# A row of constants per expert, loaded to each expert tile and added by VectorE, and made in the first layer's scan

## What is computed

```
def _L3_ffn_ref(x, W1, b1, W2, b2, Wr, br):
    E, D, H = (8, 128, 512)
    B, S = (4, 512)
    indices = jnp.argmax(softmax(x @ Wr + br), axis=-1)
    out = jnp.zeros_like(x)
    for i in range(E):
        mask = (indices == i)[..., None]
        xi = x * mask
        h = jax.nn.relu(xi @ W1[i] + b1[i])
        out = out + (h @ W2[i] + b2[i])
    return out
```

## Time and profile before

| | before |
|---|---|
| median of 3 runs | 2878.7 us |
| lowest, highest | 2875.16, 2884.09 us |
| the profiled execution, time | 2880.42 us |
| the profiled execution, span | 2878.8 us |
| granted TensorE clock, mean | 0.869 |
| PE busy, whole span | 2282.3 us (79%) |
| DVE, ACT, POOL busy | 1646.9, 1246.8, 728.6 us |

### The profile page before, as it was taken

The page is one execution under the profiler, slowest core; times in us unless marked ns, Lnnn a source line. Parts: engine busy times, 40 slices in busy tenths (PEclk is TensorE's granted clock), DMA queues, the critical chain, the costliest instruction groups (busy, mean ns, idle before and its releaser), DMA issues. The chain is left out here.

```text
span 2878.8 us, 44649 instructions
## 1 busy us (share of the span) xinstructions
PE 2282.3 (79%) x15600; PEld 1322.9 (46%) x15600; DVE 1646.9 (57%) x3299; ACT 1246.8 (43%) x1904; POOL 728.6 (25%) x872
## 2 busy tenths in 40 slices
PE   3888888852899989999755389999999788786485
PEld 2555555541344444444342134444443676454375
DVE  6676767630577747657039277777776243554202
ACT  2343434320366656665620036565656443232143
POOL 1435343441010101000000223232322112664422
PEclk8898888875799999999855589999999999996688
DMA  2111100012011101110010302121211696111075
GB/s 61 38 53 53 46 2 2 2 26 73 2 50 42 53 27 28 50 36 20 1 31 0 101 19 74 49 74 48 74 50 38 221 315 218 42 41 27 30 253 172
DMA packets 138636, 183.14 MB, mean 64 GB/s; under 512 B 26378, under 2 KB 112603, under 8 KB 133311
## 3 DMA queue, kind: packets, MB, share of 16 engines
q1 hardware_dynamic: 97629, 134.91, 15.9%
q0 software_dynamic: 13696, 32.02, 3.5%
q10 hardware_dynamic: 27126, 13.75, 1.7%
HBM read 127.86 MB, written 52.21 MB: 63 GB/s over the span
## 5 line engine op out<-in xcount | busy, mean ns | idle before, releaser
L1711 DVE TENSOR_REDUCE a_mpart<-a_mx 128x1 f32<-128x512 f32 (+3 forms) x1216 | 741.8, 656 | 293.2 <-PE a_mx L1482 156.7
L1625 ACT ACTIVATE a_prob<-a_st 128x1024 f32<-128x1024 f32 (+3 forms) x768 | 607.2, 812 | 493.1 <-PE a_st L1508 372.2
L1482 PE MATMUL a_mx<-a_ka,a_qa 96*128 96x512 bf16 (+3 forms) x1536 | 432.4, 342 | 30.7 <-DVE a_mpart L1711 14.1
L1505 PE MATMUL a_st<-a_qa,a_ka 96*128 96x512 bf16 (+3 forms) x1536 | 417.5, 334 | 30.6 <-ACT a_prob L1625 22.0
L1523 PE MATMUL a_acc<-a_prob,a_v_aug 128*9 128x512 f32 (+3 forms) x3072 | 322.0, 495 | 0.0
L1482 PEld LDWEIGHTS a_mx<-a_ka,a_qa 96*128 96x128 bf16 x1536 | 141.7, 100 | 317.7 <-DVE a_mpart L1711 172.0
L1409 POOL DMA_INDIRECT x_rows<-l_xn,l_slots x128 | 125.4, 980 | 404.9 <-ACT a_prob L1625 395.0
L1505 PEld LDWEIGHTS a_st<-a_qa,a_ka 96*128 96x128 bf16 x1536 | 146.3, 100 | 137.1 <-ACT a_prob L1625 38.2
L1508 PE MATMUL a_st<-w_mask_t,identb 128*128 128x128 bf16 x1024 | 208.8, 223 | 0.0
L2076 PE MATMUL t_psu<-t_xsT,t_w 128*128 128x128 f32 x960 | 149.2, 289 | 25.4 <-DMA t_w<-in_l_experts 17.4
L1485 PE MATMUL a_mx<-w_mask_q,identb 128*128 128x128 bf16 x768 | 165.8, 225 | 0.0
(11 more groups left out here) (444 smaller groups left out, 4129.8 us busy)
## 6 DMA issues: line engine op xcount, KB each, us to landing
t_w<-in_l_experts SPq DMA_DIRECT2D x160, 192.0 KB, 4.2
t_w<-in_l_experts SPq DMA_DIRECT2D x40, 514.0 KB
a_qa<-q_parts_dram SPq DMA_DIRECT2D x96, 192.0 KB
a_ka<-k_parts_dram SPq DMA_DIRECT2D x96, 192.0 KB
x_rows<-zeros SPq DMA_DIRECT2D x25, 512.0 KB, 3.6
t_xs<-x_rows ACTq DMA_DIRECT2D x40, 256.0 KB, 4.6
y_rows<-t_y POOLq DMA_DIRECT2D x40, 256.0 KB
q_parts_dram<-a_parts SPq DMA_DIRECT2D x24, 256.0 KB, 3.0
```

What stands on the lines that cost most here:

```text
L1482: ins = pe.matmul(to, qa[G % NQ][:, h0 + k, qi * P:(qi + 1) * P], ka[G % NQ][:, h0 + k, lo:hi], start=not masked_first, stop=k == per - 1 ...
L1505: ins = pe.matmul(to[:, lo:HALF], ka[G % NQ][:, h, j * P:(j + 1) * P], qa[G % NQ][:, h, ch * HALF + lo:(ch + 1) * HALF], start=True, stop= ...
L1625: act.activation(prob[:, v % NP_, 2 * pair:2 * pair + 2, lo:HALF], sring[s % 2][:, :, lo:HALF], ACT.Exp, scale=1.0 if alibi else scale).th ...
L1711: dve.tensor_reduce(mpart[:, G % 2, h0:h0 + per, qi, piece], slot[:, 0:per * width].rearrange("p (k w) -> p k w", k=per), X, ALU.max).then ...
```

## The change

The constants are made at the end of the first layer's scan, and handed to the experts in another way.

- In the scan, SP loads the W2 of experts 0 to 3 (1024 KB) into a third of `lmat` that the scan no longer needs, b1 and b2 beside it; after job `("base", 0)` has read it, the W2 of experts 4 to 7. ACT takes the relu of b1 (event `above`, position 57.4). PE makes the eight own rows in two jobs of 16 calls, `("base", 0)` at position 58.0 and `("base", 1)` at 60.1, and DVE copies each job's 512 numbers out of its PSUM slot. At 60.8 DVE adds b2, sums over the experts and subtracts, which gives for each expert `base - own_e` (three instructions on one partition). SP stores the 8 rows to `base_dram`. The store of the row numbers into `x3_rows` moves to here as well, and stands before the end of the scan's block.
- `route` of layer 2 loses all its work on constants, and `layer_norm` the three loads. The `ones_row` and `l3_base` tiles are gone.
- In the experts of layer 3 the call L2089 and the load of the negated row are gone. Instead SP loads for each tile the 512 bytes of its expert's row to all 128 partitions (`to_broadcast([P, D])`, 64 KB written per tile), two such loads behind the weights of tiles 3, 5 and 7 and two more at the end. Before the two, SP waits until the pair's addition in the iteration before is done. DVE adds these rows in place of `l3_base`, after a wait for their loads.

```diff
+        put(NTILES - 6.6, ("above",))
+        put(NTILES - 6.0, ("base", 0))
+        put(NTILES - 3.9, ("base", 1))
+        put(NTILES - 3.2, ("base_sum",))
...
+                    sp.wait_ge(wlast_s, NTILES // HT - 2)
+                    for done in (mm_s, gs, cd_s, st_s):
+                        sp.wait_ge(done, NTILES - NT)
+                    sp.dma_start(l3_w2, a["l3_w2"][:, 0:E3 // 2]).then_inc(w2_in[0], 16)
+                    sp.dma_start(above[:], a["l3_b1"]).then_inc(base_in, 16)
+                    sp.dma_start(l3_b2, a["l3_b2"].rearrange("(o e) d -> o e d", o=1)).then_inc(base_in, 16)
+                    sp.wait_ge(*made("base", 0))
+                    sp.dma_start(l3_w2, a["l3_w2"][:, E3 // 2:]).then_inc(w2_in[1], 16)
+                    sp.wait_ge(base_s, 1)
+                    sp.dma_start(base_dram.rearrange("(o e) d -> o e d", o=1), base_rows).then_inc(base_stored, 16)
...
+                        elif kind == "base":
+                            pe.wait_ge(above_s, 1)
+                            pe.wait_ge(w2_in[e[1]], 16)
+                            for k in range(E3 // 2):
+                                for m in range(CH):
+                                    ins = pe.matmul(slot[0:1, 0, k * D:(k + 1) * D], above[:, e[1] * E3 // 2 + k, m:m + 1], l3_w2[:, k, m],
+                                                    start=m == 0, stop=m == CH - 1)
+                            ins.then_inc(ring_made, 1)
...
+                        elif kind == "base_sum":
+                            dve.wait_ge(*freed_of("base", 1))
+                            dve.wait_ge(base_in, 32)
+                            link(dve.tensor_tensor(l3_b2, l3_b2, own, ALU.add))
+                            link(dve.tensor_reduce(own_sum[:], l3_b2.rearrange("p e d -> p d e"), X, ALU.add))
+                            dve.tensor_tensor(base_rows, own_sum[:].unsqueeze(1).to_broadcast([1, E3, D]), own, ALU.subtract).then_inc(base_s, 1)
...
-                        pe.matmul(psb, ones8[:], b2[:], start=True, stop=False)
-                        for e in range(E3):
-                            for m in range(CH):
-                                pe.matmul(pso[e // 4][:, e % 4 * D:(e % 4 + 1) * D], b1[:, e, m:m + 1], w2[:, e, m],
-                                          start=m == 0, stop=m == CH - 1)
-                                ins = pe.matmul(psb, b1[:, e, m:m + 1].to_broadcast([P, P]), w2[:, e, m],
-                                                start=False, stop=e == E3 - 1 and m == CH - 1)
...
                             e = bass.ds(chosen[k], 1)
                             sp.dma_start(w[:, k], weights[e].rearrange("e p k -> p (e k)")).then_inc(w_loaded[k], 16)
-                            if not gated:
-                                sp.dma_start(negc[:, k], negc_dram[e]).then_inc(w_loaded[k], 16)
+                            if bases is not None and k >= 3 and k % 2:
+                                base_pair(it, k // 2 - 1, chosen)
+                        if bases is not None:
+                            base_pair(it, pairs - 1, chosen)
...
-                        pe.wait_ge(w_loaded[k], (16 if gated else 32) * (it + 1))
+                        pe.wait_ge(w_loaded[k], 16 * (it + 1))
...
-                            pe.matmul(to, ones_row[:], negc[:, k], start=True, stop=False)
...
-                            dve.tensor_tensor(y[:, half, at:at + 2], made_y, base[:].unsqueeze(1).to_broadcast([P, 2, D]), ALU.add
-                                              ).then_inc(y_out, 1)
+                            dve.wait_ge(base_loaded[q], 32 * (it + 1))
+                            dve.tensor_tensor(y[:, half, at:at + 2], made_y, base[:, 2 * q:2 * q + 2], ALU.add).then_inc(y_out, 1)
```

98 lines of the change are left out of this document (43 added, 55 removed).

## The result

| | before | after |
|---|---|---|
| median (20 runs each) | 2873.93 us | 2884.32 us |
| lowest, highest | 2867.80, 2884.09 us | 2870.34, 2891.82 us |
| ratio after / before, 95% interval | | 1.003 (1.0016 to 1.0043) |
| the profiled execution: time, span | 2880.42, 2878.8 us | 2888.05, 2886.4 us |
| granted TensorE clock, mean | 0.869 | 0.865 |

The change makes the kernel slower by 0.3%, some 9 us: between 4.6 and 12.4 us by the interval. The forecast was 4.7 us faster, with no measurable change as the likeliest class. The 2884.3 us lie inside the stated range of 2865 to 2886, but by luck: the range was set from a kernel before of 2878.7 us, and over more runs this takes 2873.9. As a change, the range was -13.7 to +7.3 us, and +8.6 lies outside it.

The account below looks back on a forecast made before the run. TensorE was taken to bound the experts and the scan's end, with DMA 19% behind in the experts. Experts -12.0, scan +8.1, normalization -0.8 and routing 0 gave -4.7 us: 2874.0 us against a median of 2878.7, range 2865 to 2886.

Parts of the forecast that it names:

- What bounds the kernel: Layer 3's experts and the first scan's end: TensorE bounds, 20.00 of 20.00 us in an expert iteration, DMA share 0.81.
- By TensorE alone the stage gains 14.8 us.: Layer 3's experts: removing the 0.42 us call from 40 tiles gives 16.8 us, less 2.0 at the loop's turns.
- I take 0.26, between the two queues' prices, since they are counted in packets of this very size.: Layer 3's experts: each 64 KB row load costs 0.26 us of all DMA engines, with ends of 0.2 and 0.6.
- The second rival: Layer 3's experts: dear rows make them DMA-bound and the kernel slower, 2893 us at 0.8 us per row; chance 0.09.
- The halfway case: Rows at 0.36 to 0.6 us, or a scan costing 10 us or more: 0 to +8 us, about 2882; chance 0.15.
- 32p - 11.4: Whole kernel: change in us if a row costs p us of all DMA engines; the sign turns at p = 0.36.
- But the slots let SP run up to 8 tiles ahead, and some 1.1 us per iteration is partly taken from that lead.: Layer 3's experts: SP's lead partly covers the DMA excess, so the gain is 12 us, between 10.4 and 14.8.
- VectorE's and SP's new waits, "nothing": Layer 3's experts: VectorE's wait for the rows and SP's wait for the earlier addition of the pair cost nothing.
- signs of being wrong: Iterations at or above 20 us, `l_hmax` less than 4 or more than 10 us late, or VectorE waiting for `t_base`.
- The scan, 8.1 us: First scan's end: two jobs add 3.7 and 3.9 us and a copy 0.5, making `l_hmax` and the end 8.1 us later.
- "Nothing" for `base_sum`: First scan's end: its three one-partition instructions, 3.7 us in all, lie behind `l_hmax` beside POOL's work and cost nothing.
- Normalization -0.8, routing 0: Layer 2: three loads less in the normalization give -0.8 us (0 to -0.8); removing the routing's 65 constant calls gives 0.

Follow-up runs that it names:

- both together: Rows read from 128 places, constants made in layer 2's routing, input loads issued two tiles earlier, against the kernel before: ratio 0.993, median 2852.08 us, stage 88.52 us.

## Why the prediction was wrong, point by point

- **What bounds the kernel.** Right: TensorE in the experts and at the scan's end. What it left out was how near the third party was. The inputs' load landed after 4.4 us and had 6.3 us until TensorE wanted it (issued at 2784.46, transposed at 2790.72 in the trace of before), and the text never priced it.
- **"By TensorE alone the stage gains 14.8 us."** Too low. The call's 0.42 us was right, but a tile without it is 0.6 us shorter, so 40 tiles give some 24 us, and an iteration needs some 15.2 us of TensorE (20.03 less 8 x 0.60), not 17.2. The kernel "both together" has iterations of 16.4 us. The 15.2 are below the text's own 16.2 us of the DMA engines per iteration, so by its sum these would bound the stage even with rows that cost nothing.
- **"I take 0.26, between the two queues' prices, since they are counted in packets of this very size."** The failed step. A row costs 0.53 us by its packets, since all are read from one DRAM row; from 128 places it costs 0.22, near the 0.23 that the text read from the input loads. So the likeness of size holds for pieces from different places, and not for these. The second rival named the reason ("all 128 pieces are read from the same 512 bytes in DRAM"). The halfway case, with rows at 0.36 to 0.6 and 0 to +8 us, came nearest to what happened, and had a chance of 0.15. By the text's formula, 32p - 11.4, the price of 0.53 gives +5.6 us where 0.26 gives -3.1, so engine time alone explains some 9 of the 16 us by which the forecast missed. In the runs the dear rows cost more, 18.7 us of the stage (118.0 against 99.2 with the rows from 128 places). With rows from 128 places the stage is 11 us shorter than before, close to the forecast's 12, but by luck: TensorE's saving is larger and the late inputs take a part of it back.
- **"But the slots let SP run up to 8 tiles ahead, and some 1.1 us per iteration is partly taken from that lead."** The second failed step, to which the rest belongs. The lead belongs to the weights. The inputs have no such lead, and what fills the DMA engines by bursts delays them: they land 10.0 us after issue. The runs with rows in one iteration and with none show it: 110.5 and 99.5 us, against some 86 (110.2 - 24) by TensorE's saving alone. The first iteration, which was to gain 3.4 us, lost 0.8.
- **VectorE's and SP's new waits, "nothing".** VectorE waited once for rows, for 2.8 us, one of the text's own signs of being wrong; so was an iteration above 20 us. A wait for `t_w` in each iteration, which it expected of a stage bound by the DMA engines, didn't come.
- **What a stall costs** was not in the sum at all: in the stall shown above, the clock at 0.50 behind it doubled it.
- **The scan, 8.1 us.** The term was near, 6.98 at the end of the stage, and `l_hmax` 6.8 late. Jobs 3.65 instead of 3.9 us, the copy 0.68 instead of 0.5. "Nothing" for `base_sum` was wrong in kind: it doesn't queue, it slows POOL, by 1.7 us in two pairs.
- **Normalization -0.8, routing 0**: the first as forecast, the second within 0.4 us.
- **The sum.** 5.4 + 7.0 - 0.8 = +11.6 us by the stages of the profiled executions, against +8.6 (4.6 to 12.4) by the runs. The miss of 16.3 us between -4.7 and +11.6 is 17.4 in the experts' term, -12 against +5.4, less 1.1 in the scan's.

## What to carry to other kernels

A transfer that spreads one row over the partitions is not priced by its bytes or pieces: where it is repeated in a loop that uses the DMA engines at 80%, as here, try writing the row out once to 128 places and reading these. What the removal of a call saves is read from the start of the group before it to the start of the group behind it, in a kernel with and one without it, and not from its own time alone. Before a step of the bounding engine is shortened, list every load that must land within the loop with its time from issue to use; the one with the least slack can become the bound, as the inputs did here, and a stall can cost TensorE its clock too. Work placed on a full engine's path (the scan) cost nearly its full length, 7.0 us for two jobs of 3.65 and a copy of 0.68; where it was hidden before, its removal gave nothing.

## What the runs showed of the hardware that was not expected

- One load of 64 KB in 128 pieces of 512 bytes takes 0.34 to 0.57 us of all 16 DMA engines (means over the 40 rows of a stage) when all are read from one 512-byte row, and 0.22 when they are read from 128. Most packets take 27 ns either way; of those from one row 8 to 22% take over 200 ns on the mean. The input loads' pieces of 516 bytes take 0.24 per 128. The Trainium skill (DMA: Bandwidth & Descriptors, "Measured (HBM→SBUF, 128 partitions, SWDGE, issued from GpSimd)") has 0.95 us for 64 KB, as the time span of a load issued by GpSimd; the figures here are shares of the engines' time within a stream of loads that SP issues, and no run here measures the page's case.
- With the one-partition matmul call between them, the groups of eight on both sides take 0.98 and 0.99 us from start to start, and without it 0.90 and 0.89.
- VectorE's instructions on a single partition of 1024 numbers slow POOL's products beside them from 2.05 to 2.96 us a pair. One with two inputs took 1.96 us itself beside POOL's products, and 1.61 where these had ended.
- TensorE's granted clock fell to 0.50 behind an idle time of 3.2 us and stayed there for 6 us of full work.
